# A Mamba-style decoder layer on one core: all projection tiles of a step ahead of the turning transposes, and the taps ahead of the turned copy

## The reference

```python
h = x * rsqrt(mean(x * x) + EPS) * norm_w
proj = einsum('bsd,od->bso', h, in_proj_w)
gate, hBC, dt = proj[..., :8192], proj[..., 8192:18432], proj[..., 18432:]
hBC = silu(causal_conv(hBC, conv_w, conv_b))           # 4 taps along the tokens
hid, B, C = split(hBC)                                 # 8192, 8 x 128, 8 x 128
M = einsum(C, B) * exp(segsum(A * dt))                 # scores times decays, chunks of 128
y = einsum(M, hid * dt) + states of the chunk before + D * hid
y = group_rms_norm(y * silu(gate)) * gnorm_w
x = x + y @ out_proj_w.T
```

## Time and profile before

| | |
|---|---|
| median of 3 runs | 813.29 us (812.0 to 814.38) |
| the profiled execution | 810.53 us, of which the span from first to last instruction 808.7 us |
| granted TensorE clock, mean | 0.993 |
| busy: TensorE, VectorE, GpSimd, ScalarE | 97%, 89%, 73%, 67% of the span |
| one pass of the loop (8 steps) | 89.8 us |

### The profile page before, as it was taken

How to read it: one execution, slowest core, us unless ns; L and a number is a source line. 1 busy time by engine, 2 the same in 40 slices (tenths; PEclk the granted TensorE clock), 3 DMA queues, 4 the chain that set the end, 5 groups by cost and what they waited for, 6 DMA issues and landing times.

```text
span 808.7 us, 14439 instructions
## 1 busy us (share of the span) xinstructions
PE 785.3 (97%) x4244; PEld 615.2 (76%) x4244; DVE 720.3 (89%) x928; ACT 544.1 (67%) x1129; POOL 591.4 (73%) x484
## 2 busy tenths in 40 slices
PE   7979999999999999999999999999999999999988
PEld 6757877778777878778887778777887777777554
DVE  7999999989899988898999989998999989998763
ACT  4576675776757677676667776776667777886343
POOL 6288877787797877887788877797778876786100
PEclk9989999999999999999999999999999999999999
DMA  7453444434433444424443344432444445521001
GB/s 221 126 213 128 151 158 144 147 126 157 168 124 127 152 156 169 158 102 143 169 164 122 117 156 169 169 128 105 169 169 148 150 162 178 183 79 40 1 1 53
DMA packets 44050, 111.13 MB, mean 137 GB/s; under 512 B 5748, under 2 KB 6644, under 8 KB 44020
## 3 DMA queue, kind: packets, MB, share of 16 engines
q1 hardware_dynamic: 44020, 110.76, 40.2%
HBM read 109.30 MB, written 1.44 MB: 137 GB/s over the span
## 4 chain that ended last, share of the span: by engine, by line
PE 86%; DVE 9%; issue 2%; ACT 1%; DMA 1%; POOL 0%; DVEq 0%; ACTq 0%; SPq 0%
PE ps_in L1292 16%; PE ps_in L1293 15%; PE ps_in L1294 15%; PE ps_y L1405 8%; PE ps_o L1292 7%; PE ps_o L1294 7%; PE ps_o L1293 7%; PE ps_y L1408 3%; PE ps_t L1367 3%; DVE hid L989 1%; PE ps_o L1586 1%; PE ps_t L1417 1%; DVE stats L1202 1%; PE ps_t L1379 1%; PE ps_o L1570 1%
## 5 line engine op out<-in xcount | busy, mean ns | idle before, releaser
L533 POOL TENSOR_TENSOR w_lo<-raw,w_hi 128x512 fp32r<-128x512 f32 x144 | 234.3, 1648 | 102.8 <-ACT w_hi L642 101.6
L1292 PE MATMUL ps_in<-h_hi,w_hi 128*128 128x512 f32 x560 | 225.9, 403 | 0.0
L1293 PE MATMUL ps_in<-h_lo,w_hi 128*128 128x512 f32 x560 | 219.1, 391 | 0.0
L1294 PE MATMUL ps_in<-h_hi,w_lo 128*128 128x512 f32 x560 | 218.7, 391 | 0.0
L697 ACT ACTIVATE e<-e,nag 128x256 f32<-128x256 f32 (+1 forms) x512 | 183.5, 443 | 4.5 <-DVE nag L1059 4.5
L989 DVE SCALAR_TENSOR_TENSOR hid<-ps_in,curc,hid 128x510 f32<-128x510 f32 x186 | 138.3, 744 | 4.5
L1292 PEld LDWEIGHTS ps_in<-h_hi,w_hi 128*128 128x128 f32 x560 | 105.4, 188 | 31.1 <-issue 10.6
L564 POOL TENSOR_TENSOR e<-e,gm 128x512 f32<-128x512 f32 x64 | 100.5, 1571 | 33.2 <-DVE gm L1033 29.2
L1294 PEld LDWEIGHTS ps_in<-h_hi,w_lo 128*128 128x128 f32 x560 | 105.4, 188 | 22.7
L1293 PEld LDWEIGHTS ps_in<-h_lo,w_hi 128*128 128x128 f32 x560 | 105.6, 189 | 19.7
L662 ACT ACTIVATE hid<-ps_in,curc 128x512 f32<-128x512 f32 x62 | 48.1, 777 | 104.1 <-PE ps_in L1294 104.0
(11 more groups left out here) (237 smaller groups left out, 1204.5 us busy)
## 6 DMA issues: line engine op xcount, KB each, us to landing
e<-acs_rows SPq DMA_DIRECT2D x64, 768.0 KB, 4.5
raw<-in_w_in SPq DMA_DIRECT2D x144, 256.0 KB, 4.7
rawo<-in_w_out SPq DMA_DIRECT2D x64, 256.0 KB, 3.9
craw<-in_ctx SPq DMA_DIRECT2D x8, 256.0 KB, 4.7
res<-in_x SPq DMA_DIRECT2D x4, 256.0 KB, 3.9
out_x<-res SPq DMA_DIRECT2D x4, 256.0 KB, 2.2
acs_rows<-z SPq DMA_DIRECT2D x3, 128.0 KB, 2.0
rawo<-in_w_dt SPq DMA_DIRECT2D x1, 256.0 KB, 5.3
```

Source lines behind the costliest of these rows:

```text
L533: pool.tensor_tensor(w_lo[:, slot, :], raw[:, slot, :], w_hi[:, slot, :].bitcast(F32), ALU.subtract).then_inc(s_lo, 1)
L1292: pe.matmul(dst, lh, rh, start=first, stop=False)
L1293: pe.matmul(dst, lh, rl, start=False, stop=False)
L1294: return pe.matmul(dst, ll, rh, start=False, stop=last)
```

## The change

TensorE's step makes its h tile, the B or C tile if there is one, and the gate tile one after the other, and only then the turning and the outputs. VectorE's step does the taps of the h tile before the turned copy. No instruction, size or buffer changes. Group 0's hand-written start, up to step 3, and the end after the last step stay as they are.

```diff
@@ VectorE, step(n, t)
                     dve.wait_ge(s_ou, CT * n)
                     for k in range(TT):
                         add_output(k)
+                taps(n, ("h", t))
                 turned(*lagged(n, t, 1))
-                taps(n, ("h", t))
                 if is_first(n):
                     start_residual(t - FIRST_STEPS)
                 skip_and_gate(*lagged(n, t, 2))
@@ TensorE, step(n, t)
                 tiles = step_tiles(n, t)
-                project(*tiles[0])
+                for tile in tiles:
+                    project(*tile)
                 turn(*lagged(n, t, 1))
                 outputs(*lagged(n, t, 2))
-                for tile in tiles[1:]:
-                    project(*tile)
                 if t == 1:
                     scores(n)
```

## The result

The changed kernel takes 893.67 us (median of 4 runs, 890.72 to 894.04) where the kernel before takes 812.64: a ratio of 1.0998, 95% interval 1.0969 to 1.1026, 81 us slower. The profiled execution took 890.72 us, its span is 888.9, which is 80.2 more than before. The time lies in the predicted range, 19 us above the predicted 875.

The account below looks back on a forecast made before the run. TensorE alone was taken to set the 89.8 us pass. Stalls of 50 us in six passes, 6.3 in group 0 and 6 in the last group made 62; 810.5 + 62 + 2.8 gave 875 us, range 850 to 895.

Parts of the forecast that it names:

- step 7: Eighth step of a loop pass; the copy of the conv parameters adds about 0.3 us, stall taken as 0.5 us.
- The closed loop 4.90 + D: Gate tile, turning, outputs, VectorE's D, next gate tile's bank; against TensorE's 10.27 us step, D over 5.37 us stalls TensorE.
- D: VectorE's time from the start of `skip_and_gate` to the end of the next step's `gated`; 5.88 us measured in an ordinary step.
- steps 1, 3, 4 and 6: Steps of a pass by where the skip runs; TensorE stalls taken as 0.7, 1.1, 2.8 and 2.8 us.
- D in ordinary steps, 5.6 taken: Steps without a B or C tile: D between 4.84 and 6.5 us, taken as 5.6, a stall of 0.2.
- D behind B and C tiles, 8.2 taken: Steps 4 and 6, taps between gating and SiLU: D 7.2, 8.2 or 8.8 us; stall taken 2.8 each.
- Step 5, 0.2 taken: Treated as an ordinary step of the pass: TensorE stall 0.2 us taken, 0 low, 0.7 high.
- The clock: Rival: TensorE's clock falls in each of the 14 B and C steps, +49 us, 924 us; chance 0.05.
- the 50 of the sum: Stall predicted for the six loop passes together: 8.3 us a pass, 50 us, between 26 and 75.
- Not slower: Rival: VectorE reaches `gated` within 5.37 us of the outputs in every step, time stays 813 us; chance 0.03.
- Full waits, and a knock-on: Rival: D stays as measured everywhere and late `z` pushes casts, splits and exps too; 905 us, chance 0.11.
- No lost turns: Rival: D falls to its shortest, only steps 1, 3, 4 and 6 stall; 844 us, chance 0.08.

Follow-up runs that it names:

- short splits: GpSimd's split of the projection weights cut to 128 of 512 columns: 806.26 us in the kernel before (ratio 0.9931), 853.90 us in the changed kernel (ratio 1.0510).
- the run with filled waits: Changed kernel plus seven unused matmuls between h tile and gate tile in steps 5 and 7 of groups 0 to 6: 887.06 us, ratio 1.0915.

## Why the prediction was right, and where it was off

**TensorE sets the pass before, and the slack is small.** Right for the pass: short splits left it at 90.1 us. The 2.3 us in front of the gate tile are not all that counts, though: one more copy of 0.68 us a step lost 19 us in the old order, with TensorE waiting for the decay product in front of the outputs, a way whose slack the prediction doesn't measure.

**TensorE's order costs nothing in itself, the taps ahead of the turned copy neither.** The second half is shown by the run of VectorE's half alone (811). For the first: in step 7 of the pass without a fall, where TensorE has no wait, out tile, h tile, gate tile, turning and outputs take 10.29 us (420.83 to 431.12), against the 10.27 of the old order.

**The closed loop 4.90 + D.** Right where it binds. The hand-overs were 0.12 and 0.13 us instead of twice 0.10. It holds TensorE up behind the skips of steps 1, 3, 4 and 6, 20 times in 40 steps, and not in most of them, as the prediction had it.

**D in ordinary steps, 5.6 taken.** Too high. In the pass without a fall D is 5.13 in step 7, 5.41 in step 0 and 4.75 in step 5. The gating takes its shortest, 0.69 us, in steps 5 and 7, and 1.27 in step 0. It cost the sum little, since a D under 5.37 gives a stall of nothing: steps 0 and 7 together took 20.9 us where 21.3 were predicted. Steps 1 and 3 took 26.1, as predicted.

**D behind B and C tiles, 8.2 taken.** This term was mis-sized, and it is the largest single part of the 19 us. I let one of the measured waits for GpSimd go, since a longer step frees GpSimd earlier. The gating did lose its wait (0.69 at 480.10), but `z_low` got one of 1.1 us, which my sum did not have: the splits start some 2.4 us after the gating ends (480.79 to 483.14, and 496.29 to 498.65), and the taps push `z_low` just behind their start. D stayed at 8.82 and the steps took 13.9 us instead of 13.1, 14 times, some 11 us. The 8.8 was my high value.

**Step 5, 0.2 taken.** Mis-sized too, at 0.9, and of another cause: with D at 4.75 the loop gives no stall there. TensorE waits 0.58 us for the taps of h (the row of `hid` in the waits), whose bank the gate tile of a C step takes. The prediction names this dependence and prices it in neither B nor C steps. In a B step the B tile's wait for `gated` comes before it, in a C step nothing hides it.

**The clock.** I had it as a rival with 14 falls and 0.05. What came is between: four falls in the six passes (windows around 187, 317, 490 and 692 us) and one before them near 112, 1.6 us each in the passes; the run with filled waits took 6.6 us less. It is true that the pieces are short (0.93 and 2.10 us), and the clock fell in spite of that, behind four of twelve. The Trainium skill, "TensorE: Matmul & The Clock Gate", "HAM oscillation — how this bites in real kernels", describes a kernel that goes back to the slow clock at every one of its gaps. The run with one more copy agrees with that (gaps of 0.93 and 3.77 us, twelve of twelve); the changed kernel agrees only that repeated gaps can cost the clock.

**The total.** Skips of step 2 bound the six passes, at 138.80 and 679.33 us before and at 150.66 and 757.79 after:

```profile
138.80 0.74 DVE L1073 SCALAR_TENSOR_TENSOR z<-hid,curs,ps_y 128x512 f32<-128x512 f32 x1
...
679.33 0.74 DVE L1073 SCALAR_TENSOR_TENSOR z<-hid,curs,ps_y 128x512 f32<-128x512 f32 x1
```

```profile
150.66 0.75 DVE L1073 SCALAR_TENSOR_TENSOR z<-hid,curs,ps_y 128x512 f32<-128x512 f32 x1 [0.77 <-PE ps_y L1408]
...
757.79 0.75 DVE L1073 SCALAR_TENSOR_TENSOR z<-hid,curs,ps_y 128x512 f32<-128x512 f32 x1 [0.77 <-PE ps_y L1408]
```

The six passes gave 66.6 us, of which 6.4 (four times 1.6) for the clock. Without it they are at 60 against the 50 of the sum, and the two mis-sized terms account for the difference: twice 0.8 and 0.7, less the 0.4 that step 7 gave back, times six, is 11. Of the other 13.6 us of the span, 11.9 lie ahead of the passes, where the sum had 6.3, and 1.7 behind them, where it had 6. That their total came near the 12.3 of the sum is luck: the start was taken at half of what it cost, the last group at over three times.

**The signs and the rivals.** Two of the signs named for a wrong prediction came, though the time is in the range: the granted clock left 1.00 in the loop, and a wait that was priced nowhere, for the taps of h, showed up on TensorE. VectorE was to wait less at the start of a step; its wait in front of the turned copy doubled. "Not slower" is excluded as expected. "Full waits, and a knock-on" (905) has the D of the B and C steps right. "No lost turns" has right which steps stall for `gated` (1, 3, 4 and 6) and the D of step 5, and misses the time by its D of 7.2 behind B and C tiles. The rival of the run with one more copy, that VectorE has slack since it is busy only 78%, is refuted behind B and C tiles and comes near elsewhere.

What stays open is why the clock fell in some passes of the changed kernel and not in others with the same steps, and what made up the 11.9 us ahead of the passes.

## What to carry to other kernels

A reorder that adds no work can close a loop between two in-order engines: write down, for each buffer that a moved instruction needs, the whole way from its last writer through both engines and back, and compare its length with the step. Slack is a property of such a way, not of an engine's busy share: VectorE, at 91% in the steady pass before, did the h taps in another place for nothing and lost 19 us to a copy of 0.68 us a step. When work is moved or added, look at what it lands behind and what it pushes on: the B and C taps moved ahead of the turned copy gave back 50 us, the decay product moved behind the h taps cost 47.

## What the hardware showed that was not expected

- `z_low`, a VectorE instruction of 0.75 us with two SBUF inputs, took up to 1.79 us when it came behind the start of a GpSimd split, in every step behind a B or C tile that was read; in the old order its median is 0.747 us, with single ones up to 1.79. The added copy, with one SBUF input and 0.68 us long, took 1.79 us in the same place. Instructions that read PSUM (the taps, 0.745 us, and the skip, 0.74) kept their length throughout, at most 0.75.
- TensorE's granted clock fell to its lower level after two gaps of 0.93 and 2.10 us with a tile of 3.0 us between them, in one pass and not in the next. Where the second gap was 3.77 us it fell every time. Seven otherwise useless matmuls in the gap of 2.10 us kept it up in the passes and made the kernel 6.6 us faster.
